# Turning the attention output to feature order with VectorE's 32x32 block transposes instead of TensorE

## What is computed

```
# layer 0 (pass 0): self attention with a key mask, a gate from the context, MLP
t   = layer_norm(x);  q,k,v = t@Wq.T+bq, t@Wk.T+bk, t@Wv.T+bv
p   = softmax(q_h . k_h / 4 + (1-mask)*-1e9)            # per head h
o   = concat_h(p_h @ v_h);  x = x + o@Wo.T + bo + ctx@Wg.T + bg
x   = x + relu(layer_norm(x)@W1.T + b1)@W2.T + b2
# layer 1 (pass 1): causal self attention, no MLP
x   = x + mha(ln(x), ln(x), causal)
# layer 1 (pass 2): attention over the context, then MLP
x   = x + mha(ln(x), ctx);  x = x + relu(ln(x)@w1+b1)@w2 + b2
```

## Time and profile before

| | |
|---|---|
| time, median of 3 runs | 1781.6 us (1781.28 to 1782.33) |
| profiled execution, first to last instruction (its own time) | 1774.2 us |
| PE busy | 1538.9 us (87%) |
| DVE busy | 1308.8 us (74%) |
| ACT busy | 1142.2 us (64%) |
| POOL busy | 756.7 us (43%) |
| mean granted TensorE clock | 0.953 |
| chain that ended last | PE 62%, DMA 13%, DVE 8%, SP's queue 6% |

### The profile page before, as it was taken

One profiled execution on the slowest core, in us unless ns is written; L12 is line 12 of the kernel. 1 busy time (PEld: TensorE's weight loads), 2 busy tenths in 40 slices (PEclk: granted clock), 3 DMA queues, 4 the chain that ended last, 5 costly groups with the idle time before them and its releaser, 6 DMA issues.

```text
span 1774.2 us, 44905 instructions
## 1 busy us (share of the span) xinstructions
PE 1538.9 (87%) x14016; PEld 1308.4 (74%) x14016; DVE 1308.8 (74%) x4125; ACT 1142.2 (64%) x2737; POOL 756.7 (43%) x626
## 2 busy tenths in 40 slices
PE   2789999999999998777767767788999999999997
PEld 1578888888888887555655555567888888888876
DVE  2778788788788888776766757777787787877762
ACT  1677667776667666565665656666666766766661
POOL 3345444555445555332222223333445554454423
PEclk8799999999999999998988989899999999999998
DMA  6667655577665578667585766857555665656600
GB/s 137 136 108 98 100 90 100 93 109 99 92 98 92 102 100 127 121 106 109 96 100 90 115 99 109 129 91 107 85 99 78 108 96 80 101 86 103 84 25 13
DMA packets 292307, 173.42 MB, mean 98 GB/s; under 512 B 15696, under 2 KB 291536, under 8 KB 292176
## 3 DMA queue, kind: packets, MB, share of 16 engines
q1 hardware_dynamic: 292176, 171.98, 61.5%
HBM read 121.59 MB, written 50.33 MB: 97 GB/s over the span
## 4 chain that ended last, share of the span: by engine, by line
PE 62%; DMA 13%; DVE 8%; SPq 6%; issue 6%; POOL 3%; ACT 2%; DVEq 0%; ACTq 0%; POOLq 0%
PE d_ps L391 24%; PE t_ps L466 12%; DMA k_stack<-parts 11%; PE d_ps L613 8%; PE s_ps L450 7%; PE o_ps L484 7%; SPq L353 3%; SPq L358 2%; DMA parts<-q_part 2%; PE m_ps L398 2%; PE m_ps L506 2%; DVE prob L790 2%; ACT prob L648 1%; DVE prob_t L936 1%; POOL k_f L972 1%
## 5 line engine op out<-in xcount | busy, mean ns | idle before, releaser
L648 ACT ACTIVATE prob<-prob,neg_max 128x256 f32<-128x256 f32 (+1 forms) x1024 | 435.4, 477 | 285.2 <-DVE neg_max L790 281.7
L466 PE MATMUL t_ps<-ident_sb,prob 128*128 128x128 f32 x2816 | 455.0, 281 | 14.7 <-DVE prob_t L936 13.9
L450 PE MATMUL s_ps<-k_stack,q_stack 96*128 96x256 bf16 (+1 forms) x1536 | 296.1, 276 | 173.0 <-DMA k_stack<-parts 98.6
L466 PEld LDWEIGHTS t_ps<-ident_sb,prob 128*128 128x128 f32 x2816 | 342.8, 145 | 39.7 <-issue 31.3
L450 PEld LDWEIGHTS s_ps<-k_stack,q_stack 96*128 96x128 bf16 x1536 | 105.5, 100 | 290.9 <-issue 120.6
L648 ACT ACTIVATE prob<-s_ps,neg_max 128x256 f32<-128x256 f32 x512 | 216.9, 484 | 108.1 <-DVE neg_max L777 102.2
L936 DVE COPY prob_t<-t_ps 128x512 f32<-128x512 f32 (+1 forms) x384 | 244.9, 638 | 1.4 <-PE t_ps L466 1.4
L790 DVE CUSTOM_DVE_ANT_0 prob<-s_ps,causal 128x128 f32<-128x128 f32 (+1 forms) x512 | 159.2, 351 | 109.4 <-PE s_ps L450 73.4
L790 DVE CUSTOM_DVE_ANT_0 prob<-s_ps,bias_sb 128x256 f32<-128x256 f32 x512 | 193.5, 417 | 60.2 <-PE s_ps L450 50.8
L753 ACT ACTIVATE prob_t<-t_ps 128x512 f32<-128x512 f32 (+1 forms) x384 | 215.9, 562 | 32.0 <-PE t_ps L466 31.6
L972 POOL TENSOR_TENSOR h_lo<-h_f,h_hi 128x512 fp32r<-128x512 f32 x128 | 164.8, 1288 | 131.9 <-DVE h_hi L868 131.9
(11 more groups left out here) (105 smaller groups left out, 3664.9 us busy)
## 6 DMA issues: line engine op xcount, KB each, us to landing
q_stack<-parts SPq DMA_DIRECT2D x288, 128.0 KB, 5.1
k_stack<-parts SPq DMA_DIRECT2D x288, 128.0 KB, 8.9
parts<-q_part SPq DMA_DIRECT2D x96, 192.0 KB, 2.3
parts<-k_part SPq DMA_DIRECT2D x96, 192.0 KB, 2.4
c_in<-ctx SPq DMA_DIRECT2D x32, 256.0 KB, 8.2
x_in<-x_mid SPq DMA_DIRECT2D x32, 256.0 KB, 3.7
x_res<-x_mid SPq DMA_DIRECT2D x32, 256.0 KB, 3.9
x_in<-x SPq DMA_DIRECT2D x16, 256.0 KB, 3.9
```

The costliest lines, as they stand in the source:

```text
L450: last = mm(s_ps[:, h % 2, q * S:q * S + n], q_stack[:, t.par, h, q * P:(q + 1) * P], k_stack[:, t.par, h, 0:n], start=True, stop=True)
L466: last = nc.tensor.transpose(t_ps[:, h % 2, c:c + P], prob[:, h % 4, q, k * P:(k + 1) * P], ident_sb[:, :])
L648: last = nc.scalar.activation(prob[:, h % 4, q, 0:n], src, ACT.Exp, bias=neg_max[:, h % 4, q:q + 1], scale=-1.0)
```

## The change

The trip through token order is dropped. Each head stays in its own 32 partitions, and 32x32 blocks are turned by DVE in place of the full 128x128 turns by PE:

- DVE transposes each chunk of `o_ps` (128x256, from PSUM) block by block into `o_q`, in slots 1, 5, 9 and 13, as the first thing of the slot. ACT's four copies go.
- In slot 6 DVE takes one reciprocal (128x32) and multiplies twice (128x256 each), now with both operands in SBUF, into `o_n`, where two chunks' 16 features lie side by side in a block of 32.
- In slot 7 DVE transposes `o_n` back (128x512, SBUF to SBUF) into `o_f`; `ot_hi` is cast from it in slot 8 and `ot_lo` subtracted in POOL's slot 10, ahead of `rstd`.
- PE's twelve transposes for each task and ACT's copy to `tf_a` go. The order of heads is permuted by `HEAD` in the scores and values, so that features come out in their own order.
- Waits for `m_ps` and `tf_a` are adapted.

```diff
+HEAD = tuple(8 * (c // 2) + 2 * j + c % 2 for c in range(CH) for j in range(CH))
 # PE
-                    last = mm(s_ps[...], q_stack[:, t.par, h, q * P:(q + 1) * P], k_stack[:, t.par, h, 0:n], ...)
+                    last = mm(s_ps[...], q_stack[:, t.par, HEAD[h], q * P:(q + 1) * P], k_stack[:, t.par, HEAD[h], 0:n], ...)
-                if h in (6, 8) and has(st.prev):
-                    head_tokens(st, (h - 6) // 2)
-                if h == 10 and has(st.prev):
-                    pe.wait_ge(o_norm.sem, o_norm.after(st.prev))
-                    flip(m_ps, o_sb).then_inc(o2t_mm.sem, 1)
 # ACT
-                if h % CH == 1:
-                    t, c = chunk_at(st, h, PV_LAG + 1)
-                    if t is not None:
-                        act.wait_ge(pv_mm.sem, pv_mm.after(t, c + 1))
-                        nc.scalar.activation(o_t[:, c, :], o_ps[:, 0:S], ACT.Copy).then_inc(o_done.sem, 1)
-                if h == 11 and has(st.prev):
-                    nc.scalar.activation(tf_a[:, :, :], m_ps[:, :]..., ACT.Copy).then_inc(ot_f.sem, 1)
 # DVE
-                if h in (7, 9) and has(st.prev):
-                    v.reciprocal(rden[:, q, :], o[:, :, HD]).then_inc(rden_done.sem, 1)
-                    v.tensor_tensor(o_sb[:, q, :]..., o[:, :, 0:HD], rden[:, q, :]..., ALU.mult)
+                if h % CH == 1:
+                    t, c = chunk_at(st, h, PV_LAG + 1)
+                    if t is not None:
+                        dve.wait_ge(pv_mm.sem, pv_mm.after(t, c + 1))
+                        if c == 0 and st.prev:
+                            dve.wait_ge(o_norm.sem, o_norm.after(st.prev))
+                        v.transpose(o_q[:, c].rearrange("p b w -> p (b w)"), o_ps[:, 0:S]).then_inc(o_done.sem, 1)
+                if h == 6 and has(st.prev):
+                    dve.wait_ge(o_done.sem, o_done.after(st.prev))
+                    v.reciprocal(rden[:, :, :], o_q[:, :, :, HD]).then_inc(rden_done.sem, 1)
+                    dve.wait_ge(rden_done.sem, rden_done.after(st.prev))
+                    for g in range(KC):
+                        last = v.tensor_tensor(o_n[:, g].rearrange("p b (c d) -> p c b d", d=HD),
+                                               o_q[:, 2 * g:2 * g + 2, :, 0:HD],
+                                               rden[:, 2 * g:2 * g + 2].unsqueeze(3)
+                                               .to_broadcast([P, 2, S // BLK, HD]), ALU.mult)
+                    last.then_inc(o_norm.sem, 1)
+                if h == 7 and has(st.prev):
+                    dve.wait_ge(o_norm.sem, o_norm.after(st.prev))
+                    v.transpose(o_f[:, :, :].rearrange("p k s -> p (k s)"),
+                                o_n[:, :].rearrange("p k b w -> p (k b w)")).then_inc(ot_f.sem, 1)
-                if h == 12 and has(st.prev):
+                if h == 8 and has(st.prev):
                     dve.wait_ge(ot_f.sem, ot_f.after(st.prev))
-                    v.tensor_copy(ot_hi[:, :, :], tf_a[:, :, :]).then_inc(ot_h.sem, 1)
+                    v.tensor_copy(ot_hi[:, :, :], o_f[:, :, :]).then_inc(ot_h.sem, 1)
 # POOL
-                if h == 12 and has(st.prev):
+                if h == 10 and has(st.prev):
                     pool.wait_ge(ot_h.sem, ot_h.after(st.prev))
-                    sub(ot_lo[:, :, :], tf_a[:, :, :], ot_hi[:, :, :], ot_l.sem)
+                    sub(ot_lo[:, :, :], o_f[:, :, :], ot_hi[:, :, :], ot_l.sem)
```

More of the change, by code:

```diff
@@ L39 @@
 CH = 4
+BLK = 32
 NPASS = 3
@@ L449, in scores @@
                     n = (q + 1) * P if t.p == 1 else S
-                    last = mm(s_ps[:, h % 2, q * S:q * S + n], q_stack[:, t.par, h, q * P:(q + 1) * P],
-                              k_stack[:, t.par, h, 0:n], start=True, stop=True)
+                    last = mm(s_ps[:, h % 2, q * S:q * S + n], q_stack[:, t.par, HEAD[h], q * P:(q + 1) * P],
+                              k_stack[:, t.par, HEAD[h], 0:n], start=True, stop=True)
                 last.then_inc(s_mm.sem, 1)
@@ L483, in values @@
                         h = CH * c + j
-                        last = mm(o_ps[32 * j:32 * j + VW, lo:S], v_sb[:, t.par, k, h, :],
+                        last = mm(o_ps[32 * j:32 * j + VW, lo:S], v_sb[:, t.par, k, HEAD[h], :],
                                   prob_t[:, h % 8, k * S:k * S + S - lo], start=(k == 0), stop=(k == TT - 1),
@@ L487, in values @@
                 last.then_inc(pv_mm.sem, 1)
[L489 to L507, removed]
-                last.then_inc(ot_mm.sem, 1)
             def slot(st, h):
@@ L519, in slot @@
                         pe.wait_ge(xt_f.sem, xt_f.after(st.nxt))
-                    else:
-                        pe.wait_ge(ot_f.sem, ot_f.after(st.old))
+                    elif has(st.older, MLP):
+                        pe.wait_ge(x2t_f.sem, x2t_f.after(st.older))
                     flip(m_ps, x2_hat).then_inc(x2t_mm.sem, 1)
@@ L618, in slot @@
                     pe.wait_ge(x_hat.sem, x_hat.after(st.nxt2))
-                    if st.prev:
-                        pe.wait_ge(ot_f.sem, ot_f.after(st.prev))
+                    if has(st.prev, (0,)):
+                        pe.wait_ge(ct_f.sem, ct_f.after(st.prev))
+                    elif has(st.nxt2, (2,)):
+                        pe.wait_ge(ct_f.sem, ct_f.after(st.nxt2))
+                    elif has(st.old, MLP):
+                        pe.wait_ge(x2t_f.sem, x2t_f.after(st.old))
                     elif st.nxt:
@@ L739, in slot @@
                     act.wait_ge(xt_mm.sem, xt_mm.after(st.nxt2))
-                    if st.prev:
-                        act.wait_ge(ot_l.sem, ot_l.after(st.prev))
-                    elif st.nxt:
+                    if st.nxt:
                         act.wait_ge(xt_l.sem, xt_l.after(st.nxt))
```

37 lines of the change are left out of this document (12 added, 25 removed).

## The result

| | before | after |
|---|---|---|
| time, median of 4 runs each | 1781.4 us (1780.6 to 1782.3) | 1829.7 us (1828.1 to 1833.2) |
| ratio, 95% interval | | 1.0278 (1.0263 to 1.0293): slower |
| profiled execution, first to last instruction | 1774.2 us | 1829.1 us |
| PE / DVE / ACT / POOL busy | 1538.9 / 1308.8 / 1142.2 / 756.7 us | 1523.8 / 1394.3 / 1065.8 / 751.1 us |
| mean granted TensorE clock | 0.953 | 0.919 |

48.3 us slower, where 30 were forecast; 1829.7 lies inside the range. The difference of the two spans is 54.9. In every execution whose time and span are both known, about 2 us lie around the span (1.9 to 2.9; 1831.05 and 1829.1 here). The 7.4 us of before were therefore not all "around" it: its profiled execution was some 5 us quicker than its median run.

What follows compares the result with a forecast made beforehand. It took PE's work to bound passes 0 and 2, and a chain through k's casts and `k_stack`'s landing pass 1. Terms +35 - 10 + 4 + 2 - 1 = +30 on 1781.6 gave 1812 us, range 1786 to 1840.

Steps and rivals of the forecast that it cites:

- the forecast's own: Whole kernel: the range of the main forecast without its rivals, 1796 to 1828 us, chance 0.58.
- Prices: DVE's new instructions: 128x256 transpose 0.35 us, 128x512 0.62, reciprocal 0.35, each multiply 0.35 plus one wait of 0.4.
- the rule it cites: Slot 6, pass 1: two-SBUF-input DVE instructions contend with GpSimd SBUF reads, the later blocks; first multiply waits 0.8 us.
- Pass 1: Transpose and multiplies delay k's casts, so `k_stack` reads start 2.2 us later a step: +35 us, bounds +27 to +50.
- the second branch: Slot 6, pass 1: k's second cast comes 2.7 us later, 0.35 is slack, so reads start 2.3 us later.
- Pass 0: PE wants 1.3 us a step, DVE's added work lets 0.7 through: 15 steps, -10 us, bounds -20 and +8.
- Pass 2: DVE's guard of head 9 comes 0.1 to 0.9 us later: +0.3 a step, 13 steps, +4 us, bounds -13 and +18.
- Ends: First steps, where scores also wait for DMA, +2 us; the tail, with PE's transposes on its way, -1.
- DVE as the bound everywhere: Rival: transposes at high prices add 1.2 us a step to DVE's stretch; 1860 us, or 1835 for half; chance 0.18.
- PE's time through whole: Rival: DVE's net addition stays under its idle, passes 0 and 2 gain 20 and 13 us; 1774 us, chance 0.08.
- Slack in the chain: Rival: only 1 us a step arrives in pass 1, +16 with -10 elsewhere, making +4 us; chance 0.08.
- POOL's lock on the multiplies: Rival: each multiply waits a whole POOL difference, 1.13 to 1.27 us; about +55 us, 1837, chance 0.08.

Runs made afterwards that it cites:

- e2: e1 with the reciprocal and both multiplies behind k's second cast and ct_hi in slot 6, in all passes: 1801.0 us, ratio 1.0132.
- e11: Changed kernel with the reciprocal and both multiplies behind k's second cast in pass 1 alone, chunk 3's transpose still first in slot 5: 1816.3 us, ratio 1.0214.
- e1: Changed kernel with chunk 3's block transpose moved behind k's first cast, L844 and the copies of v in slot 5: 1803.7 us, ratio 1.0157.
- e12: e1 with twelve identity transposes a task given back to TensorE in slots 6, 8 and 10: 1829.9 us, ratio 1.0295.
- e6: e1 with 24 identity transposes on TensorE at the end of slot 15 in pass 1's 16 waiting steps: 1795.2 us, ratio 1.0078.
- e7: e6 with reciprocal and multiplies late in pass 1 alone, and five identity transposes ahead of slot 1's scores in pass 2: 1765.0 us, ratio 0.9925.
- e8: e7 with ACT instead of DVE copying head 5's turned probabilities in passes 0 and 2: 1746.0 us, ratio 0.9813.
- e9: e8 without the five identity transposes in slot 1 of pass 2: 1736.6 us, ratio 0.9771.
- e4: Changed kernel with 36 identity transposes on TensorE at the end of slot 15 in pass 1's waiting steps: 1804.5 us, ratio 1.0144.
- e3: Changed kernel with twelve identity transposes a task given back to TensorE in slots 6, 8 and 10: 1821.8 us, ratio 1.0245.
- e5: Kernel before with 24 identity transposes on TensorE at the end of slot 15 in pass 1's 16 waiting steps: 1762.2 us, ratio 0.9897.
- e10: Kernel before with e5's 24 identity transposes and ACT's copy of head 5's probabilities in passes 0 and 2: 1767.2 us, ratio 0.9940.

## Why the prediction was right, and where its sum was short

The mechanism was right: the transpose that waits for chunk 3 took over the place ahead of k's first cast, and pass 1 pays for it. The sum was 30 us and 48 were measured (55 in the profiles). The time lies inside the stated range and 2 us above the forecast's own, 1796 to 1828. The terms of passes 0, 1 and 2 were each too low, by 10, 12 and 6 us in the profiles, that of the first steps by 2, and only the tail made up 4. By its steps:

- **Prices.** The 128x256 transpose took 0.45 us, 0.37 between starts (taken: 0.35); the 128x512 0.695 us, 0.62 between starts (0.62); the reciprocal 0.345 (0.35); the pair of multiplies 1.23 in the step shown, 0.76 where POOL rests, so one wait of 0.47 (0.4). All near the taken values. DVE's busy time rose by 85.5 us, not 105; 17.6 of the difference is `x_in`, which meets POOL less often. The 0.8 that the prediction gives for this wait by the rule it cites is a slip: by its own times the multiply's turn comes at 915.67 and POOL's last q part ends at 914.42 + 1.71 = 916.13, which makes 0.46. So the rule fits the measurement.
- **Pass 1, mis-sized: 2.2 us a step taken, 2.94 measured, +47 instead of +35.** On average over the 16 steps, k's first cast comes 2.16 us later after the first scores (1.71 taken), from it to the end of POOL's last k part are 0.51 more (0.5 taken), and from there to the next scores 0.27 more (0 taken). The middle term is right: L837 follows L820 by 3.39 us (3.5 foretold), and the chain goes through POOL's k part, the second branch. What is missing is 0.45 ahead of the cast, 0.29 of it in slot 2, which took 2.99 us instead of 2.70 with the clock at half for longer, and a landing of `k_stack` that takes longer (10.86 in the step shown against 10.56). The prediction held TensorE's clock and the landing constant. e2 and e11 give the two places 1.9 and 1.0, each with its share of the clock's part.
- **Pass 0, wrong: -0.7 us a step taken, none measured, 0 instead of -10.** Slots 6, 7 and 8 did become shorter by 0.33, 0.11 and 0.19 us. The step that failed is "the slots after it are long on PE ..., so what is gained is kept": slot 10 grew from 2.64 to 2.95, as its product waited 16 times, 6.5 us in all, for ACT's `h_f`, a wait that before didn't have, and the rest went in slots 0, 11 and 15, by up to 0.1 each. ACT stands behind exponentials, and these behind DVE's guards; that it is this chain is argued from their order. The count of DVE's work stopped at slot 8's copy; it should have gone on to the next thing that PE needs of DVE or ACT. e1 and e12 show that the full 1.23 was there to be had.
- **Pass 2: +0.3 a step right, the total not: +9.7 instead of +4.** An undisturbed step is 37.0 against 36.7, as foretold. Three stretches at half clock, of 1.5 us each (38.5 against 37.0), and the first step, 40.7 us against 38.3 with 9.5 us at half clock against 4.9, make up 7 us; the prediction had no term for them. The last step gave 0.9 back.
- **Ends.** The first steps cost 3.2 and 0.5 (+2 taken), the tail gave 4.9 (-1 taken). PE's turns, ACT's copies and the waits between them are all on its way; no run takes it apart.
- **The 7.4 us around the span** were 2, and 5 of run to run.
- **What the profile would show.** 547 us between tasks 18 and 34, not 535. PE's wait for `k_stack` grew by 28.9 us, not by more than 35; the rest went into its waits for DVE's guards (26.5 to 55.4), behind which PE stood in the slots between.
- **Rivals.** DVE as the bound everywhere (1835 to 1860): prices refute it, though its neighbour, DVE's lateness in pass 0, is what ate PE's gain. PE's time through whole: it needs the transpose elsewhere, which e1 shows in pass 0 (-1.0 a step). Slack in the chain: refuted. POOL's lock on the multiplies: each time for the first of the two, by some 0.4 us, and not a whole difference. The 55 us of that rival count little of its own "+1 in the others": with 15 and 13 steps it would be some 74.

Open: what decides about the long steps and the falls of the clock in pass 2. There are two kinds. In e1, e2, e6, e7 and e12 every second step is long; it begins with DVE's standstill and comes with the instruction transfers, and depends neither on TensorE's transposes (e12) nor on the five added ones (e7). ACT's copy removed it twice (e8, e9). Why the order of instructions brings the transfers is open. In after, e4 and e11 the clock falls in every third step, for 3.4 us and with no such transfers, and with TensorE's work given back (e3) it doesn't; before, e5 and e10 don't have it either. Why in every third step, while PE's wait ahead of it is the same in all, is open.

## What to carry to other kernels

Price a new instruction by where it stands in its engine's fixed order and not by its length: here 0.45 us of transpose, put ahead of a cast that others wait for, cost 1.9 us a step because it waits for something that the cast does not. When work is taken from the bound engine and given to another, follow the stretch on to the next thing that the bound engine needs of that other engine, or of a third behind it; the saving of 1.23 us was there to be had, and the 0.6 of it that came was lost again from slot 10 on. When DVE or another engine stands still ahead of an instruction whose inputs are there, look whether the profile's instruction queue has transfers at that time, before blaming the clock. And measure a change after mending its order: the same idea was 2.8% slower as written, and 1.7% faster than its equal when reordered.

## What the runs showed of the hardware that was not expected

- The instructions of a loop with two steps in its body seem to be loaded anew each time round in some orders: 25 more transfers of kind "instruction" in pass 2 (32 against 7), with DVE standing still for 1.8 and 2.05 us at their times and the step 3.5 us longer at full clock (e7), up to 6.4 with the clock falling behind it (43.6 against 37.2 in e12). One moved DVE instruction brought it (after to e1), one copy taken from DVE in each step removed it (e7 to e8).
- In the changed kernel, PE busy for 34.1 of 37.0 us a step, the clock fell to half for 3.4 us in every third step, which cost 1.5 us each time.
- 24 or 36 transposes of an identity in TensorE's idle time, thrown away, made both kernels faster (1.0% and 1.3%).
- DVE's 32x32 block transpose of float32 runs like a copy: 128x256 from PSUM in 0.44 us, 128x512 in SBUF in 0.70.
- A DVE multiply with both inputs in SBUF took 0.42 us alone and 1.2 on average beside POOL's subtractions in e2; a float32 to bf16 cast of 128x512 0.41 alone and 1.28 during a POOL subtraction of 1.16 us (e11).
